# Graph attention and max pooling on one core: ranked groups redrawn, a dense product over 28 tiles, and small work moved between engines

## The reference, cut to what matters

```python
# layer 0
h = relu(layernorm(x));  H = h @ W.T + b;  s = H @ a_s;  r = H @ a_r
e = leaky_relu(adj * s + adj * r.T, 0.2)
x = x + softmax(where(adj > 0, e, -9e15), axis=1) @ H
# layer 1
h = relu(layernorm(x));  y = h @ weight
out = relu(adj @ y + bias)
pooled[i] = max over j with adj[i, j] != 0 of out[j]
x = x + pooled
```

## Time and profile before

| | us |
| --- | --- |
| median of 3 runs | 2652.41 (2651.3 to 2653.63) |
| the profiled execution | 2656.13 |
| its span | 2654.4 |
| VectorE busy | 1494.6 (56%) |
| GpSimd busy | 1565.4 (59%) |
| TensorE busy | 990.8 (37%) |
| ScalarE busy | 379.5 (14%) |

### The profile page before, as it was taken

How to read it: one execution, slowest core, us unless ns; L and a number is a source line. 1 busy time by engine, 2 the same in 40 slices (tenths; PEclk the granted TensorE clock), 3 DMA queues, 4 the chain that set the end, 5 groups by cost and what they waited for, 6 DMA issues and landing times.

```text
span 2654.4 us, 20418 instructions
## 1 busy us (share of the span) xinstructions
PE 990.8 (37%) x4772; PEld 571.1 (22%) x4772; DVE 1494.6 (56%) x4088; ACT 379.5 (14%) x1166; POOL 1565.4 (59%) x1620
## 2 busy tenths in 40 slices
PE   3664254444456654416469999400000000000000
PEld 1441143211234422416324444200000000000000
DVE  6888988888465564644665555176736741012211
ACT  1541054300223322214200000000000000000000
POOL 0001675027277757777466574377757777667776
PEclk8987677767777777657679999755555555555555
DMA  9999887579998997334432232422242222222121
GB/s 349 404 366 395 279 286 270 238 294 328 329 369 318 318 362 264 73 76 118 132 87 62 60 88 57 109 61 59 75 48 52 52 54 53 48 49 54 52 52 46
DMA packets 158194, 450.37 MB, mean 170 GB/s; under 512 B 34738, under 2 KB 82692, under 8 KB 125172
## 3 DMA queue, kind: packets, MB, share of 16 engines
q1 hardware_dynamic: 81972, 313.26, 31.5%
q0 software_dynamic: 53344, 114.94, 18.9%
q10 hardware_dynamic: 22752, 20.82, 2.5%
HBM read 409.76 MB, written 39.12 MB: 169 GB/s over the span
## 4 chain that ended last, share of the span: by engine, by line
POOL 40%; issue 17%; PE 15%; DVE 13%; DVEq 6%; DMA 5%; SPq 3%; POOLq 0%; ACT 0%; ACTq 0%
POOL ring L658 23%; PE psV L1070 13%; POOL ring L586 12%; DMA a_buf<-in_adj 3%; DVE words L1196 2%; DVEq L1195 2%; POOL out L664 2%; POOL y_table L599 1%; DVE words L1187 1%; DVE words L1191 1%; DVEq L1190 1%; SPq L400 1%; PE psV L899 1%; DVE found L1220 1%; SPq L387 1%
## 5 line engine op out<-in xcount | busy, mean ns | idle before, releaser
L586 POOL DMA_INDIRECT ring<-h_table,srec x523 | 512.1, 979 | 234.3 <-issue 157.1
L658 POOL DMA_INDIRECT ring<-p_table,srec x554 | 535.7, 967 | 189.0 <-issue 167.5
L1308 DVE TENSOR_TENSOR ring<-ring 128x128 f32<-128x128 f32 (+6 forms) x302 | 147.9, 490 | 560.1 <-DMA ring<-p_table,srec 405.1
L899 PE MATMUL psV<-a_buf,bit_ident 128*128 128x512 bf16 x1024 | 299.2, 454 | 245.4 <-DMA a_buf<-in_adj 175.4
L955 PE MATMUL psH<-ring,ident 128*128 128x128 f32 x1046 | 188.8, 355 | 294.3 <-ACT trec L754 136.2
L955 PEld LDWEIGHTS psH<-ring,ident 128*128 128x128 f32 x1046 | 178.9, 266 | 308.6 <-issue 241.8
L1070 PE MATMUL psV<-rec_all,a_buf 128*128 128x512 bf16 x1008 | 223.0, 380 | 0.0
L1080 PE MATMUL psH<-ones_row,flag_col 128*1 128x1 f32 x2 | 0.2, 163 | 587.2 <-DVEq L1537 587.2
L621 POOL DMA_INDIRECT ring<-y_table,srec x177 | 173.0, 977 | 56.6 <-issue 56.0
L899 PEld LDWEIGHTS psV<-a_buf,bit_ident 128*128 128x128 bf16 x1024 | 109.9, 110 | 418.6 <-issue 255.2
L572 POOL DMA_INDIRECT records<-rec_all,rank x63 | 63.2, 1003 | 165.4 <-DVEq L1273 146.8
(11 more groups left out here) (228 smaller groups left out, 2020.3 us busy)
## 6 DMA issues: line engine op xcount, KB each, us to landing
a_buf<-in_adj SPq DMA_DIRECT2D x256, 1024.0 KB, 12.0
ring<-p_table,srec POOLq DMA_INDIRECT x554
ring<-h_table,srec POOLq DMA_INDIRECT x523
packed<-wbuf ACTq DMA_DIRECT2D x32, 256.0 KB, 7.7
a_buf<-packed SPq DMA_DIRECT2D x8, 1024.0 KB, 6.4
trec<-records ACTq DMA_DIRECT2D x63, 128.5 KB, 3.3
h_table<-stage POOLq DMA_DIRECT2D x16, 258.0 KB, 8.0
a_buf<-r_row SPq DMA_DIRECT2D x1, 4096.0 KB, 18.9
```

The lines of the kernel that those rows point to most:

```text
L586: pool.indirect_dma_start(ring[:, A_AT[q] + j, :], None, h_table, bass.IndirectOffsetOnAxis(srec_u[g][:, i, LIST + j:LIST + j + 1], 0)).th ...
L658: pool.indirect_dma_start(ring[:, C_AT[n] + j, 0:D], None, p_table, bass.IndirectOffsetOnAxis(slot, 0)).then_inc(s_rows[n % BUFS], 16)
L899: last = pe.matmul(psV[n % 2][:, h * BANK:(h + 1) * BANK].rearrange("p (g n) -> p g n", n=P), bit_ident[:, k, :], rows[:, :, k, :], start= ...
L1308: dve.tensor_tensor(ring[:, at:at + h, 0:D], ring[:, at:at + h, 0:D], ring[:, at + n - h:at + n, 0:D], op)
```

## The change

Five things change.

1. *Groups.* The streaming order and the groups become 12 to 27, 1 to 11, 28 to 47 and 48 to 63 (16, 11, 20 and 16 tiles; 16, 15, 16 and 16 before). Slots per group are 132, 188, 117 and 81 (122, 224, 95 and 82 before), so 518 h gathers instead of 523. The groups are ranked after steps 15, 26, 46 and 62 (`ENDS`; 15, 30, 46 and 62 before). `STEP` and `BEHIND` are new tables: the tile with the most slots is at step 34 (39 before), the fourth group begins at step 65 (70 before), and the last tile is at step 79 (81 before). Classes are counted per group, up to 46.
2. *Dense product* over 28 tiles, 7 batches, 56 blocks (32, 8, 64 before). 36 ranked tiles with 198 slots are summed from y gathers (32 with 177 before); 653 p gathers instead of 662. `sums_behind` now puts the last 11 sums behind the last block.
3. *Scores.* The two additions move from VectorE (`e_raw`) to ScalarE (`raw_scores`, written to `e_sc`), which now waits for the gather; VectorE waits for ScalarE. The negated maximum comes from one instruction.
4. *Norm statistics.* bn_stats, bn_aggr and the shift leave VectorE's `close`, which accumulates the row sum in its last instruction; ScalarE makes shift, sum of squares and logarithm.
5. *Lists.* `extract` writes nodes into the records; counting and conversion are done in `classify`, for the whole group.

Some tensors of the hub share space with others, and the hub's parts begin one step sooner at the end (`HUB_NORM` at 76 instead of 77) with 4 and 3 splits of y instead of 4 and 4. `hub_work` is spread over the gathers of tiles 1 to 22 instead of 1 to 25.

```diff
-GROUPS = [(16, 16, 24), (1, 15, 48), (32, 16, 24), (48, 16, 24)]
-CLASSES = 32
+GROUPS = [(12, 16, 24), (1, 11, 48), (28, 20, 24), (48, 16, 16)]
+CLASSES = [min(512 // n, 46) for _, n, _ in GROUPS]
-SLOTS = [[21, 11, 10, 9, 9, 8, 7, 7, 7, 6, 6, 5, 5, 4, 4, 3],
-         [47, 24, 20, 17, 16, 14, 13, 12, 11, 10, 10, 9, 8, 7, 6],
...
+SLOTS = [[22, 12, 11, 10, 9, 9, 8, 8, 7, 7, 6, 6, 5, 5, 4, 3],
+         [46, 24, 20, 17, 15, 14, 13, 12, 10, 9, 8],
...
-DENSE = 32
-DENSE_FROM = 31
+DENSE = 28
+DENSE_FROM = 27
-STEP = [19, 19, 20, 20, 21, 21, 22, 22, 23, 23, 24, 24, 25, 25, 26, 26, 39, 43, 45, 46, 47, 48, 49, 50, 51, 52,
...
+STEP = [18, 19, 20, 20, 21, 22, 22, 23, 23, 24, 25, 25, 26, 26, 27, 27, 34, 38, 40, 41, 42, 43, 44, 45, 46, 46,
...
-    return [m for m in range(len(Y_SLOTS)) if min((sum(Y_SLOTS[:m + 1]) + m + 8) * 9 // 32, 63) == step]
+    return [m for m in range(len(Y_SLOTS)) if min((sum(Y_SLOTS[:m + 1]) + m + 8) * 9 // 32, DENSE_BATCHES * BLOCKS - 1) == step]
...
+            def raw_scores(q):
+                g, i, k = RANKED[q]
+                s = srec[g][:, i, S:S + 1]
+                act.wait_ge(s_rows[q % BUFS], A_COUNT[q])
+                act.activation(e_sc[q % 2][:, 0:k], ring[:, A_AT[q]:A_AT[q] + k, D], ACT.Identity, bias=s)
+                act.activation(e_sc[q % 2][:, k:k + 1], srec[g][:, i, RS:RS + 1], ACT.Identity,
+                               bias=s).then_inc(s_raw, 1)
...
+                act.activation(t_shift[:, c:c + 1], x_sum[:, c:c + 1], ACT.Copy, scale=-1.0 / D).then_inc(s_shift, 1)
+                act.wait_ge(s_shift, q + 1)
                 act.activation(hn[0][:, c, :], trec[:, q % RECORDS, 0:D], ACT.Relu,
                                bias=t_shift[:, c:c + 1]).then_inc(s_tnorm, 1)
-                act.activation(t_log[:, c:c + 1], t_mv[:, c, 1:2], ACT.Ln, bias=eps_col[:, 0:1]).then_inc(s_tlog, 1)
+                act.activation(squares[:], trec[:, q % RECORDS, 0:D], ACT.Square, bias=t_shift[:, c:c + 1],
+                               accum_out=t_var[:, c:c + 1]).then_inc(s_square, 1)
...
                 for q in AT_STEP[n]:
+                    raw_scores(q)
+                for q in AT_STEP[n]:
                     exponents(q)
...
-                dve.tensor_scalar(junk[:, 0:w], found[:, 0:w], 0.0, 0.0, ALU.is_gt, ALU.add,
-                                  accum_out=degree[:, t:t + 1])
-                dve.tensor_copy(rec_u[g][:, t - GROUPS[g][0], at:at + w], found[:, 0:w])
...
+                dve.tensor_scalar(held, rec[g][:, :, lists], 0.0, None, ALU.is_gt)
+                dve.drain()
+                dve.tensor_reduce(degree[:, cols], held, AX.X, ALU.add)
+                dve.tensor_copy(rec_u[g][:, :, lists], rec[g][:, :, lists])
...
-                dve.wait_ge(s_rows[q % BUFS], A_COUNT[q])
-                dve.tensor_scalar(e_raw[:, 0:k], ring[:, at:at + k, D], s, None, ALU.add)
-                dve.tensor_scalar(e_raw[:, k:k + 1], srec[g][:, i, RS:RS + 1], s, None, ALU.add)
-                dve.drain()
+                dve.wait_ge(s_raw, q + 1)
                 e = e_sc[q % 2][:, 0:k + 1]
-                dve.scalar_tensor_tensor(e, e_raw[:, 0:k + 1], ALPHA, e_raw[:, 0:k + 1], ALU.mult, ALU.max)
-                dve.drain()
-                dve.reduce_max(m_max[:], e, axis=AX.X)
-                dve.drain()
-                dve.tensor_scalar(m_neg[q % 2][:], m_max[:], -1.0, None, ALU.mult)
+                dve.scalar_tensor_tensor(e, e, ALPHA, e, ALU.mult, ALU.max)
+                dve.drain()
+                dve.reduce_max(m_neg[q % 2][:], e, axis=AX.X, negate=True)
...
-                dve.scalar_tensor_tensor(row, psH[q % 2][:, 0:D], l_inv[:, 0:1], row, ALU.mult, ALU.add)
-                dve.drain()
-                dve.bn_stats(t_stats[:], row)
-                dve.drain()
-                dve.bn_aggr(t_mv[:, c, :], t_stats[:])
-                dve.drain()
-                dve.tensor_scalar(t_shift[:, c:c + 1], t_mv[:, c, 0:1], -1.0, None, ALU.mult)
+                dve.scalar_tensor_tensor(row, psH[q % 2][:, 0:D], l_inv[:, 0:1], row, ALU.mult, ALU.add,
+                                         accum_out=x_sum[:, c:c + 1])
```

More of the change, by code:

```diff
@@ L38 @@
 STREAM = [t for a, n, _ in GROUPS for t in range(a, a + n)] + [0]
-TAKEN = {t: 48 if t < 3 else 40 if t < 5 else 32 if t < 14 else 24 if t < 47 else 16 for t in range(1, T)}
+TAKEN = {t: 48 if t < 3 else 40 if t < 5 else 32 if t < 12 else 24 if t < 47 else 16 for t in range(1, T)}
 WIDTH = {t: TAKEN[t] if t < 40 else 16 for t in range(1, T)}
@@ L60 @@
 CHUNKS = 4
+ENDS = [sum(n for _, n, _ in GROUPS[:g + 1]) - 1 for g in range(4)]
 LOADS = [15, 22, 40, 56]
@@ L149, in hub_work @@
     work = [2] * rounds + [1] * (HUB_KEEP // 8)
-    ready = [sum(work) * min(sum(C_SLOTS[1:m + 2]) / sum(C_SLOTS[1:26]), 1) for m in (n - 1, n)]
+    ready = [sum(work) * min(sum(C_SLOTS[1:m + 2]) / sum(C_SLOTS[1:23]), 1) for m in (n - 1, n)]
     return [r for r in range(len(work)) if (n == 0 or sum(work[:r + 1]) > ready[0]) and sum(work[:r + 1]) <= ready[1]]
@@ L472, in _ @@
             for i in range(2):
-                sp.wait_ge(s_pst[i], 16 * (DENSE_BATCHES // 2))
+                sp.wait_ge(s_pst[i], 16 * len(range(i, DENSE_BATCHES, 2)))
             sp.wait_ge(s_lowst, 16)
@@ L951, in sum_slots @@
                     pe.wait_ge(s_att, q - 1)
-                pe.wait_ge(s_ranked, len([n for n in (15, 30, 46, 62) if n <= STEP[q]]))
+                pe.wait_ge(s_ranked, len([n for n in ENDS if n <= STEP[q]]))
                 pe.wait_ge(s_scaled, q + 1)
@@ L961, in count_classes @@
                 pe.wait_ge(s_onehot, g + 1)
-                closed = len([q for q in range(NR) if STEP[q] < (15, 30, 46, 62)[g]])
+                closed = len([q for q in range(NR) if STEP[q] < ENDS[g]])
                 if closed > 0:
                     pe.wait_ge(s_att, closed)
-                cols = one_hot[:, 0:CLASSES * n]
-                pe.matmul(psH[0][:, 0:CLASSES * n], upper_bf[:], cols, start=True, stop=True)
-                pe.matmul(psH[1][:, 0:CLASSES * n], ones_bf[:], cols, start=True, stop=True).then_inc(s_counted, 1)
+                m = CLASSES[g] * n
+                cols = one_hot[:, 0:m]
+                pe.matmul(psH[0][:, 0:m], upper_bf[:], cols, start=True, stop=True)
+                pe.matmul(psH[1][:, 0:m], ones_bf[:], cols, start=True, stop=True).then_inc(s_counted, 1)
             def turn_rows(n):
@@ L1008, in dense_norm @@
                 pe.wait_ge(s_hstep[l], t * 8 + 4)
-                pe.matmul(psV[0][:, D:2 * D], hub_nT[:], w1_sb[:], start=True, stop=True).then_inc(s_hstep[l], 1)
+                pe.matmul(psV[0][:, D:2 * D], hub_nT, w1_sb[:], start=True, stop=True).then_inc(s_hstep[l], 1)
             pack(0)
@@ L1232, in classify @@
                 cols = slice(a, a + n)
[L1233 removed]
+                m = CLASSES[g]
+                lists = slice(LISTS + LIST, LISTS + LIST + w)
+                held = V[:, 0:n * w].rearrange("p (t k) -> p t k", k=w)
+                dve.drain()
[3 more added lines that the diff above has]
+                dve.tensor_copy(rec_u[g][:, :, lists], rec[g][:, :, lists])
+                dve.drain()
+                dve.tensor_scalar(row_class[:, 0:n], degree[:, cols], float(m - 1), None, ALU.min)
                 dve.tensor_tensor(own[:, cols], with_own[:, cols], without[:, cols], ALU.subtract)
                 dve.drain()
[L1236 to L1238 removed]
+                dve.tensor_tensor(one_hot[:, 0:m * n].rearrange("p (c t) -> p c t", t=n),
+                                  row_class[:, 0:n].unsqueeze(1).to_broadcast([P, m, n]),
+                                  class_no[:, max(CLASSES) - m:max(CLASSES)].unsqueeze(2).to_broadcast([P, m, n]), ALU.is_equal)
                 dve.drain().then_inc(s_onehot, 1)
@@ L1400, in _ @@
                     mean_row()
[L1401 to L1402 removed]
+                if n in ENDS:
+                    classify(ENDS.index(n))
                 for q in AT_STEP[n]:
@@ L1412, in _ @@
                     dense_close(0, 0)
-                for b in SPLITS.get(n, []):
+                for _ in range(SPLITS.get(n, 0)):
                     split_y(splits)
```

110 lines of the change are left out of this document (53 added, 57 removed), and 4 rows, old and new, of the table SLOTS.

## The result

The changed kernel takes 2560.0 us in the median of 4 runs (2553.4 to 2564.0), the one before 2651.9 (2649.5 to 2653.6) beside it: ratio 0.965, 95% interval 0.9639 to 0.9662. The profiled execution took 2558.27 us, its span is 2556.3. One of the four runs of the kernel with the moves alone took 4242.94 us, at a granted clock of 1.0; its cause is not known, and it is left out of that kernel's times.

What follows compares the result with a forecast made beforehand. Four parts bound the span: VectorE's lists, GpSimd's issue of groups 1 to 3, the dense product, the p gathers. First p gather at 1598 plus 955 gives 2553, minus 2: 2551 us; range 2512 to 2600.

Steps and rivals of the forecast that it cites:

- Lists and group 1: Up to group 1's rank: cheaper lists, closes and scores and fewer tiles bring it to 474 us, 89 earlier.
- First long tile: GpSimd's wait behind the tile with most slots: it goes on at 602 us instead of 711, the wait about 35.
- Matrix: Before group 3's rank: 15 tiles still to come at 793 us, 13.4 us each, so ranked at 1017.
- matrix-bound rival: Before group 3's rank: matrix comes at 15.8 us a tile, rank at 1050, +33, total 2584 us; chance 0.15.
- The tail: Tile 47's scores to first y gather: 150.5 us becomes 182.5; hub chunks +26, hand-over to ScalarE +22, shorter closes -16.
- The other side of the hand-over: Score additions on ScalarE between steps 19 and 62: priced at zero because extractions cover them; otherwise 1.5 us a step.
- the rival that made the kernel slower: VectorE waits for ScalarE's additions in all 47 steps; at 3 us each +141, total 2692 us; chance 0.07.
- Start of the dense product: Dense product begins 15 us behind the first y gather, as before: 1266 instead of 1351.14 us.
- Dense stage: Dense start to first p gather: 332 us instead of 344; 11 late sums let only 12 of TensorE's 42 us arrive.
- the rival that TensorE ends the stage: Dense stage: late sums run faster, first p gather 5.4 us after TensorE's end, -31, total 2520 us; chance 0.07.
- The rival of a held GpSimd: Dense stage: VectorE's bit operations stop GpSimd, +100, total 2651 us, no change; chance 0.02.
- Last stage: p gathers to the end: 653 instead of 662 gives -11.5, first segment's wait +7, so 955 us.

Runs made afterwards that it cites:

- the moves alone: Old groups, slots, steps and 32-tile dense product, with score additions and norm statistics on ScalarE and lists by group: 0.9927 of the kernel before, 2632.4 us.
- f1: Changed kernel with earlier splits of y, earlier y sums and score additions back on VectorE in all steps: 0.9537 of the kernel before.
- the three edits: Changed kernel with earlier splits of y, earlier y sums and score additions back on VectorE from step 64 on: 2519.1 us, 0.9513 of the kernel before.
- the second trace: A second measurement of the unchanged new kernel, on the first chip: 0.9651 of the kernel before, span 2555.4 us.
- the tables alone: New groups, slots, steps and 28-tile dense product; score additions, norm statistics and list counting left as before: 0.9722 of the kernel before, 2575.6 us.
- the second question: Changed kernel with additions back on VectorE from step 64 (0.9591, 0.9606) or in all steps (0.9602, 0.9594), or statistics back (0.9678), against the kernel before.
- fourth question: Whether additions on ScalarE help anywhere: changed kernel with earlier splits, earlier sums and all additions on VectorE, 0.9537 of the kernel before.
- the sums moved: Changed kernel with only the y sums put earlier in VectorE's order, on another chip: 0.9629 of the kernel before.
- the e and d runs: Seven of the twelve experiments, edits of the changed kernel on two chips where the kernel before takes some 3002 us: ratios 0.9591 to 0.9678.

## Why the prediction was right, and where it was not

It gave 2551 us and a range of 2512 to 2600; 2560.0 was measured. The four parts of the span and what ends each were right. Several terms were wrong in both directions and cancelled.

*Lists and group 1.* Forecast 474, traced 476.7. The steps' sum put about 26 us of the 89 down to VectorE's cheaper work and the rest to four tiles fewer; the runs give 22.6 and 64.0. The estimate above moves some 4 us from the second to the first. Of the 22.6 the two additions have at most 4.4 (f1 against the three edits; 2.2 against the second trace of the changed kernel); the division between lists and statistics was not run on this chip.

*First long tile.* 602 against 607.9, and two errors lie behind the 6 us. The forecast let VectorE's own order set the scores, at 567. VectorE was there at 570.2, but the rows were not: ScalarE's additions began when the last of the 46 gathers had landed, 16.6 us behind the end of its issue (562.5), and VectorE's scores at 579.74, 12.7 late. The row had shown such a wait, 9.82 us for `ring`. From the scores to the sum it then took 27.9 us, not 34.7: TensorE's sum began when ScalarE was through with the rows, where before it stood behind a packing that waited 11.57 us for the matrix. ScalarE, VectorE and TensorE at this tile:

```profile
579.07 0.37 ACT L742 ACTIVATE e_sc<-ring,srec 128x46 f32<-128x46 f32 x1 [71.23 <-DMA ring<-h_table,srec]
579.74 0.21 DVE L1308 SCALAR_TENSOR_TENSOR e_sc<-e_sc 128x47 f32<-128x47 f32 x1 [9.57 <-ACT e_sc L743]
594.72 12.63 PE L971 MATMUL psH<-ring,ident 128*128 128x128 f32 x92 [5.06 <-ACT trec L762]
```

So the wait behind this tile did not shrink to 35, it was 42.81, and the 6 us were handed on up to group 2 (799.8 for 793.5).

*Matrix.* Group 3's records at 1017.3 for 1017. The 6 us were given back here: GpSimd comes to the records 2.56 us before the rank. The pace of 13.4 us a tile, an estimate between 11.5 and 15.3, held: the last extraction began at 996.6 for 994. The matrix-bound rival (1050) fell.

*The tail.* From the scores of tile 47 (1066.6) to the first y gather 181.6 us, forecast 182.5. The later hub chunks were +26 in the forecast and are +21.8 in the kernel with the tables alone (172.3 against 150.5). The hand-over less the shorter closes, 22 - 16 = +6, is +9.3 (181.6 against 172.3). That the additions lie on the path there, behind ScalarE's copies, is what the second question showed, but the two sizes were luck: on the other chips the additions cost 11 us, not 22, and the closes without statistics gave back nothing (tail 246.6 with them, 247.1 without), not 16.

*The other side of the hand-over*, priced at zero, cost nothing (fourth question); the rival that made the kernel slower fell with it.

*Start of the dense product.* This step failed: "dense product 15 later as before". It came 29.4 us behind the first y gather. Before, 8 splits of y at 2.7 us lay behind the last close. The changed table puts its second lot at the step of the last close and behind that close, so 12 fall there. VectorE's rows of the changed kernel, the last close and the first and the last split behind it:

```profile
1238.18 0.16 DVE L1334 RECIPROCAL l_inv<-l_sum 128x1 f32<-128x1 f32 x1 [1.83 <-PE psH L972]
...
1238.90 0.43 DVE L1389 CAST a_buf<-stage 128x512 bf16<-128x512 f32 x1
...
1272.69 0.43 DVE L1389 CAST a_buf<-stage 128x512 bf16<-128x512 f32 x1 [3.29 <-DMA stage<-y_table]
...
1275.36 2.04 DVE L1454 TENSOR_SCALAR wbuf<-a_buf 128x512 uint16<-128x512 uint16 x8 [0.22 <-issue]
```

Twelve such groups of four operations stand between 1238.9 and 1275.2; the first bits, for which TensorE waits, come behind them. The section on the change named the numbers of the table, and the prediction took nothing from them. The three edits cut the twelve to eight and won 12.6 us at this place (9.9 against the second trace). Alone, on another chip, this edit won 10.0 there and lost 5.0 ahead of it, in the tail.

*Dense stage.* 332 us forecast from its start to the first p gather, 326.9 traced; TensorE's 56 blocks 295 forecast, 294.5 traced. That the eleven sums behind the last block eat the gain of the shorter product was right and is shown by undoing it: 301.4, where the rival that TensorE ends the stage had 295 + 5.4 = 300.4. The rival of a held GpSimd fell: its y gathers take 947 ns in the median beside VectorE's bit operations, as before. The lock that the Trainium skill describes (SBUF — State Buffer, SBUF: two separate sides) does not show in this row; whether these bit operations are 2-port operations, no run here shows.

*Last stage.* 955 forecast, 951.8 traced. Of the +7 for the first segment's wait 3.4 us came.

In sum: the start of the dense product was 14 us too early by its own term; the y gather (3), the dense stage (5) and the last stage (3) gave 11 back, so the span was met within 3.3 us. The total is better than its terms: the long tile, the two sizes in the tail and the start of the dense product were each off by 6 to 16 us.

## What to carry to other kernels

A stage ends with its last producer, so shortening the engine that is busy there (TensorE, 44 us less here) is worth only what the other engines' last pieces of work allow (17 us here): look which items of a hand-written order stand behind the last block, and spread them before work is cut. Work that is moved to an idle engine must be placed by what stands ahead of it in that engine's order: the same additions cost nothing that could be measured under long extractions (first chip) and 9 to 11 us in a tail where the engine is in step with TensorE. When a table of such numbers changes, count what it leaves behind the last item on the path: four splits more cost 10 to 13 us there. Put ahead of it, they delayed the last closes, and only 5 us were left of the gain (on another chip).

## What was not expected of the hardware

The same program takes 2650 us on one chip and 3002 on two others. Not the instructions are slower: GpSimd's y gathers take 947 ns, a max over the word scores 1.23 us, on a chip of either kind. VectorE stands still between instructions, for nothing that the trace names. On the first chip it never does so for over 1 us, in the kernel before, the changed one or the three edits; in the kernel with the sums moved, on another chip, it does 168 times, 487 us in all, ScalarE 39 times (355 us). VectorE's rows of that kernel, first one such wait of many us, then a stretch where every third instruction has one:

```profile
1034.54 1.23 DVE L1206 MAX8 words<-psV 128x8 f32<-128x1024 f32 x1 [38.42 <-remote]
...
2290.79 0.66 DVE L1488 MAX8 a_buf<-a_buf 128x8 f32<-128x480 f32 x1 [2.07 <-issue]
2292.20 0.09 DVE L1491 MATCH_VALUE_LOAD a_buf<-a_buf 128x8 f32 x1 [0.75 <-issue]
2292.28 0.64 DVE L1491 MATCH_REPLACE8 a_buf<-a_buf 128x480 f32<-128x480 f32 x1
2294.99 0.66 DVE L1488 MAX8 a_buf<-a_buf 128x8 f32<-128x480 f32 x1 [2.07 <-issue]
```

I had taken such a kernel's time to be that of the program. The cause stays open. The Trainium skill (Runtime: NRT & Kernel Launch, Instruction fetch mechanics) says that each engine fetches its code in blocks by a DMA queue of its own and that this is mostly hidden. The traces speak against slow fetches: the packets of the two instruction queues take 1.6 us at most in this kernel and 1.7 in the changed kernel on the first chip, and none of them falls into VectorE's wait of 38.42 us. For the comparisons it means that what the e and d runs say of a few us may not hold on the first chip. The tail's differences there do not follow these waits: VectorE has 20 to 40 us of them in the tail of the four kernels with the shorter one, 23 to 37 in the other three. The dense stage's may: 149 us with the sums moved, 89 to 122 in the other six.
